# Cross-attention and expert FFN on one core: which score tiles are multiplied in three rounded terms, who copies the shift row, and the order of the last sums

## What is computed

```python
kv = context @ Wkv;  k, v = split(kv);  q = layernorm(x) @ Wq
dots = einsum('bhnd,bhmd->bhnm', q, k) * SCALE
dots = dots - (1.0 - mask)[:, None, :, None] * 1000000.0
attn = softmax(dots, axis=-1)
x = x + (einsum('bhnm,bhmd->bhnd', attn, v) heads merged) @ Wout + bout
# then: x = x + ffn(layernorm(x)), one expert (w1, b1, gelu, w2, b2) for each batch
```

## Time and profile before

| what | value |
|---|---|
| median of 3 executions | 381.06 us (379.85 to 382.0) |
| profiled execution, its time | 381.56 us |
| profiled execution, span of the trace | 379.6 us |
| mean granted TensorE clock | 0.991 of full speed |
| PE, DVE, ACT, POOL busy | 367.0, 278.7, 255.1, 115.5 us |

### The profile page before, as it was taken

The page is one execution under the profiler, slowest core; times in us unless marked ns, Lnnn a source line. Parts: engine busy times, 40 slices in busy tenths (PEclk is TensorE's granted clock), DMA queues, the critical chain, the costliest instruction groups (busy, mean ns, idle before and its releaser), DMA issues.

```text
span 379.6 us, 5788 instructions
## 1 busy us (share of the span) xinstructions
PE 367.0 (97%) x1713; PEld 280.4 (74%) x1713; DVE 278.7 (73%) x456; ACT 255.1 (67%) x334; POOL 115.5 (30%) x125
## 2 busy tenths in 40 slices
PE   7899999999999999999999999999999999999795
PEld 6667777777777787777767887777777887787555
DVE  5888577977797679787698579686789678443653
ACT  3556576797679467796679466887688466958321
POOL 1701562245225341226123431336133330022000
PEclk9999999999999999999999999999999999999988
DMA  7587277348734673359735493279636550377000
GB/s 243 202 191 174 54 145 178 85 116 157 180 82 112 115 179 57 96 130 248 169 96 126 90 205 75 59 164 230 160 92 141 93 100 10 106 147 133 12 2 6
DMA packets 30622, 47.10 MB, mean 124 GB/s; under 512 B 2011, under 2 KB 21371, under 8 KB 30608
## 3 DMA queue, kind: packets, MB, share of 16 engines
q0 software_dynamic: 9936, 27.40, 37.0%
q1 hardware_dynamic: 20672, 19.52, 17.2%
HBM read 24.59 MB, written 0.23 MB: 65 GB/s over the span
## 4 chain that ended last, share of the span: by engine, by line
PE 83%; DVE 10%; issue 3%; DMA 2%; ACT 1%; SPq 1%; DVEq 0%
PE ps_s L439 27%; PE ps_a L479 22%; PE ps_x L496 10%; PE ps_a L472 9%; PE ps_x L529 4%; PE ps_a L416 2%; PE ps_x L549 2%; DMA ctxt_raw<-in_ctx_t 2%; DVE ex_sum L889 2%; DVE shift_diag L910 1%; PE ps_x L453 1%; DVE chunk_max L899 1%; PE ps_x L558 1%; DVE ex_lo L895 1%; PE ps_x L509 1%
## 5 line engine op out<-in xcount | busy, mean ns | idle before, releaser
L899 DVE TENSOR_REDUCE chunk_max<-ps_x 128x1 f32<-128x500 f32 x168 | 110.9, 676 | 31.2 <-PE ps_x L496 28.3
L697 ACT ACTIVATE ex_all<-ps_s 125x896 f32<-125x896 f32 x96 | 88.0, 917 | 46.3 <-PE ps_s L439 44.6
L479 PE MATMUL ps_a<-ex_all,ctx_sb 125*128 125x448 f32 x248 | 110.9, 540 | 0.0
L715 ACT COPY ps_s<-shift_row 125x896 f32<-125x896 f32 x94 | 85.7, 911 | 12.6 <-DVE shift_row L1036 10.0
L496 PE MATMUL ps_x<-ctxt_hi,qk_hi 128*128 128x500 f32 x168 | 80.3, 481 | 1.7 <-DVE chunk_max L899 1.5
L1213 POOL DMA_DIRECT2D ex_all<-ex_all x48 | 42.2, 879 | 117.5 <-ACT ex_all L697 113.3
L439 PE MATMUL ps_s<-qk_hi,ctxt_hi 128*125 128x448 f32 x192 | 76.3, 479 | 0.0
L479 PEld LDWEIGHTS ps_a<-ex_all,ctx_sb 125*128 125x128 f32 x248 | 46.2, 189 | 16.8 <-issue 12.4
L439 PE MATMUL ps_s<-qk_hi,ctxt_lo 128*125 128x448 f32 x192 | 54.8, 367 | 0.0
L439 PE MATMUL ps_s<-qk_lo,ctxt_hi 128*125 128x448 f32 x192 | 54.7, 366 | 0.0
L439 PEld LDWEIGHTS ps_s<-qk_hi,ctxt_hi 128*125 128x125 f32 x192 | 35.9, 187 | 24.5 <-issue 23.4
(11 more groups left out here) (108 smaller groups left out, 385.4 us busy)
## 6 DMA issues: line engine op xcount, KB each, us to landing
ex_all<-ex_all POOLq DMA_DIRECT2D x48, 448.0 KB, 4.5
ctxt_raw<-in_ctx_t SPq DMA_DIRECT2D x8, 750.0 KB, 6.1
ctx_sb<-in_ctx SPq DMA_DIRECT2D x8, 750.0 KB
ctxt_hi<-in_ctx_t POOLq DMA_DIRECT2D x21, 250.0 KB, 3.0
w_sb<-in_w SPq DMA_DIRECT2D x4, 512.0 KB, 4.7
...
```

What stands on the lines that cost most here:

```text
L479: mm = nc.tensor.matmul(ps_a[:, c, 0:CH], ctx_sb[0:MT, u, t, :], ex(t)[0:MT, c * CH:(c + 1) * CH], start=(slot == 0), stop=(slot == TM - 1))
L697: nc.scalar.activation(half(ex(t)[0:MT, :]), src, ACT.Exp, scale=SCALE).then_inc(ex_ready, 1)
L715: nc.scalar.copy(ps_s[0:MT, t % 2, :, 0:CH], half(shift_row[0:MT, b.parity, :])).then_inc(seeded, 1)
L899: nc.vector.tensor_reduce(chunk_max[:, k, t:t + 1], filled()[:, 0:MC], AX.X, ALU.max).then_inc(job_free, 1)
```

## The change

- `SPLIT` becomes 0, 2, 4, 6, 8, 10: tiles 0 and 10 are multiplied in three rounded terms too, except tile 10 of the last batch. `ctx_hi` and `ctx_lo` hold six context tiles instead of four. `PV_ORDER` swaps its last two tiles, so tile 10 takes slot 11.
- The row sum is made as 0+9, +1, +10, +2, +11 (`SUM_PARTS`). The first addition is at (10, 2), the next two at (11, 1), the last two again at the start of the next batch.
- DVE's two copies of the shift row are gone. ACT copies both banks of `ps_x` at once into `ps_s` as the seed of the first tile (`first_seed`), then into `shift_row`, and only then counts both banks as drained. For batch 0 that seed is tile 2's.
- ACT rounds the row sum after the next batch's exponential of tile 1 instead of tile 0; it goes into `shift_diag`, no longer a buffer of its own.
- In the last batch additions come at (10, 0) and (11, 0), the first half of `last_probs_ctx` stands ahead of the sum's products, and `y_job` of half 0 uses the form that half 1 had: even heads in 64 rows of the bank, odd heads in the other 64, and one more addition on DVE to join them.
- In batch 0 `ctx_hi` is made by ACT during the setup, `ctx_lo` by POOL in step 0.

The diff, without the lines that only rename or delete a helper's body:

```diff
-    SUMS = CHAINS - 1 + TM - 1 - LAST_DMA
-    SPLIT = [2, 4, 6, 8]
-    PV_ORDER = [0, 1, 2, 3, 5, 4, 7, 6, 9, 8, 10, 11]
+    SUM_PARTS = [9, 1, 10, 2, 11]
+    SUMS = len(SUM_PARTS)
+    SPLIT = [0, 2, 4, 6, 8, 10]
+    PV_ORDER = [0, 1, 2, 3, 5, 4, 7, 6, 9, 8, 11, 10]
...
-    ADD_AT = {(10, 2): (0,), (11, 0): (1, 2)}
+    ADD_AT = {(10, 2): (0,), (11, 1): (1, 2)}
     ADD_LATE = (3, 4)
-    LAST_ADD_AT = {(10, 2): (0,), (11, 0): (1, 2), (11, 1): (3,)}
+    LOW_AT = [(t + 1, 1) for t in SPLIT[:-1]] + [(11, 0)]
+    LAST_ADD_AT = {(10, 0): (0, 1), (11, 0): (2, 3)}
...
-        sum_hi = sb("sum_hi", [P, Q], F32R)
+        sum_hi = shift_diag[:, :, :].rearrange("p t q -> p (t q)")
...
+        def buffer_free(n):
+
+            return read_by(SPLIT[n - 2]) if n >= 2 else read_by(SPLIT[SPLITS - 2 + n]) - TM
+
+        def summed(t):
+
+            return 1 + (SUM_PARTS.index(t) if t else 0)
...
-            def last_probs_ctx(b):
-
-                pe.wait_ge(ex_ready, b.at(TM, TM))
-                for c in range(2):
-                    for t in (TM - 2, TM - 1):
-                        mm = nc.tensor.matmul(ps_a[:, c, 0:CH], ctx_sb[0:MT, b.parity, t, :], ex(t)[0:MT, c * CH:(c + 1) * CH],
-                                              start=False, stop=(t == TM - 1))
-                    mm.then_inc(last_half, 1)
+            def last_probs_ctx(b, c):
+
+                for t in (TM - 2, TM - 1):
+                    pe.wait_ge(ex_ready, b.at(TM, t + 1))
+                    mm = nc.tensor.matmul(ps_a[:, c, 0:CH], ctx_sb[0:MT, b.parity, t, :], ex(t)[0:MT, c * CH:(c + 1) * CH],
+                                          start=False, stop=(t == TM - 1))
+                mm.then_inc(last_half, 1)
...
-                    if pair.half == 1:
+                    if pair.half is not None:
                         out_rows = slice(TOK * (h % 2), TOK * (h % 2) + TOK)
...
+            last_probs_ctx(last, 0)
             sum_jobs(last)
-            last_probs_ctx(last)
+            last_probs_ctx(last, 1)
...
+            def first_seed(b, t):
+
+                act.wait_ge(job_ready, jobs.value())
+                act.wait_ge(ex_ready, b.at(TM, t - 1))
+                nc.scalar.copy(ps_s[0:MT, t % 2, :, 0:CH], ps_x[0:MT, :, 0:CH]).then_inc(seeded, 1)
+                nc.scalar.copy(half(shift_row[:, b.parity, :]), ps_x[:, :, 0:CH]).then_inc(job_free, 2)
...
                     exponentials(b, t)
                     if t == 1 and b.off > 0:
+                        sum_high_part(b.later(-1))
                         att_out(b.later(-1))
-                    if t + 2 < TM:
-                        if t == 0 and first:
-                            jobs.n += 2
+                    if prepare and t == TM - 2:
+                        ex_high_part(b, SPLITS - 1)
+                    if t == 0 and first:
+                        jobs.n += 2
+                        first_seed(b, 2)
+                    elif t + 2 < TM:
+                        if t == 1 and first:
                             act.wait_ge(job_free, jobs.value())
                         seed(b, t + 2)
                     elif prepare:
                         if t + 2 == TM:
                             jobs.n = FIRST_JOBS if first else jobs.n + 2
+                            first_seed(b.later(1), 0)
+                        else:
                             act.wait_ge(job_free, jobs.value())
-                        seed(b.later(1), t + 2 - TM)
-                    if t == 0 and b.off > 0:
-                        sum_high_part(b.later(-1))
+                            seed(b.later(1), 1)
...
-                    if t in SPLIT:
+                    if t in SPLIT[:-1]:
                         ex_high_part(b, SPLIT.index(t))
...
+                if h == HEADS - BEHIND:
+                    ctx_high_part(Batch(None, 0))
                 drain_later_queries(h)
...
-                if pair.half == 1:
+                if pair.half is not None:
+                    other = slice(TOK * (1 - pair.half), TOK * (1 - pair.half) + TOK)
                     step(nc.vector.tensor_tensor(x1[r, :], bank[r, 0:D], pair.pick(x_tok)[r], ALU.add))
-                    nc.vector.tensor_tensor(x1[r, :], bank[0:TOK, 0:D], x1[r, :], ALU.add).then_inc(job_free, 1)
+                    nc.vector.tensor_tensor(x1[r, :], bank[other, 0:D], x1[r, :], ALU.add).then_inc(job_free, 1)
...
-            def shift_copies(b):
-
-                wait(dve, seeded, b.at(TM, -TM - 2))
-                for c in range(2):
-                    nc.vector.tensor_copy(shift_row[:, b.parity, c * CH:(c + 1) * CH], filled()[:, 0:CH]).then_inc(job_free, 1)
...
-                    if (at[0] - 1, at[1]) in [(t, 1) for t in SPLIT]:
-                        ex_low_part(b, SPLIT.index(at[0] - 1))
+                    if at in LOW_AT and (prepare or LOW_AT.index(at) < SPLITS - 1):
+                        ex_low_part(b, LOW_AT.index(at))
...
-                        pool.wait_ge(ex_lo_ready, b.at(SPLITS, 2))
+                        pool.wait_ge(ex_lo_ready, b.at(SPLITS, 3))
```

More of the change, by code:

```diff
@@ L472, in probs_ctx @@
                             mm = nc.tensor.matmul(ps_a[:, c, 0:CH], a[0:MT, u, n, :], e[0:MT, n % 2, c * CH:(c + 1) * CH],
-                                                  start=False, stop=False)
+                                                  start=(slot == 0 and term == 0), stop=(slot == TM - 1 and term == 2))
                     mm.then_inc(pv_done, 1)
@@ L562, in shift_jobs @@
             def shift_jobs():
-                for c in range(2):
+                for _ in range(2):
+                    c = jobs.n % 2
                     shift_rows(job()[:, 0:CH], P, c, start=True).then_inc(job_ready, 1)
@@ L687, in exponentials @@
                 if t < CHAINS:
-                    wait(act, ex_summed, b.at(SUMS, max(t, 1) - SUMS))
+                    wait(act, ex_summed, b.at(SUMS, summed(t) - SUMS))
                 elif t < CHAINS + RING:
@@ L692, in exponentials @@
                     if before > LAST_DMA:
-                        wait(act, ex_summed, b.at(SUMS, CHAINS - 1 + before - LAST_DMA - SUMS))
+                        wait(act, ex_summed, b.at(SUMS, summed(before) - SUMS))
                 else:
@@ L702, in ex_high_part @@
                 act.wait_ge(ex_ready, b.at(TM, t + 1))
-                if n >= 2:
-                    act.wait_ge(pv_done, b.at(TM, read_by(SPLIT[n - 2])))
+                wait(act, pv_done, b.at(TM, buffer_free(n)))
                 nc.scalar.copy(ex_hi[0:MT, n % 2, :], ex(t)[0:MT, :]).then_inc(ex_hi_ready, 1)
@@ L877, in add_to_sum @@
             def add_to_sum(b, n):
+                t = SUM_PARTS[n]
                 dst = ex_sum[0:MT, b.parity, :]
[L880 to L883 removed]
+                left = ex(0)[0:MT, :] if n == 0 else dst
+                if n == 0:
+                    added_by_dma(dve, b, LAST_DMA - CHAINS + 1)
+                if t < CHAINS:
+                    added_by_dma(dve, b, LAST_DMA - CHAINS + 1 + t)
                 else:
[L885 removed]
                     dve.wait_ge(ex_ready, b.at(TM, t + 1))
[L887 removed]
                 wait(dve, ex_summed, b.at(SUMS, n))
[L889 removed]
+                nc.vector.tensor_tensor(dst, left, ex(t)[0:MT, :], ALU.add).then_inc(ex_summed, 1)
             def ex_low_part(b, n):
                 dve.wait_ge(ex_hi_ready, b.at(SPLITS, n + 1))
[L894 removed]
+                wait(dve, pv_done, b.at(TM, buffer_free(n)))
                 nc.vector.tensor_tensor(ex_lo[0:MT, n % 2, :], ex(SPLIT[n])[0:MT, :], ex_hi[0:MT, n % 2, :].bitcast(F32),
@@ L1045, in drain @@
                 def drain(at):
-                    if b.off == 0 and at == FIRST_SHIFT_AT:
-                        shift_copies(b)
-                    if prepare and at == SHIFT_AT:
-                        shift_copies(b.later(1))
+                    if (b.off == 0 and at == FIRST_SHIFT_AT) or (prepare and at == SHIFT_AT):
+                        jobs.n += 2
                     if b.off == 0 and at in FOLD_AT:
@@ L1223, in iteration @@
                 for t in range(TM):
-                    if b.i is None and b.off == 0 and t == 2:
+                    if b.i is None and b.off == 0 and t == 0:
                         ctx_low_part(b)
```

12 lines of the change are left out of this document (1 added, 11 removed).

## The result

The changed kernel takes 379.34 us (median of 10 runs, 378.34 to 379.68), the kernel before 380.98 (10 runs, 379.85 to 382.64). The ratio is 0.9949, 95% interval 0.9931 to 0.9967. So 1.6 us were gained where 4.6 were forecast; the time lies just above the range. The profiled execution of after took 379.52 us (span 377.6), 2.04 less than that of before.

What follows compares the result with a forecast made beforehand. PE, busy 97% of the span and 83% of the chain, was taken as the bound. Terms summed to -4.8 us: 376.8 on the profiled execution's 381.56, 376.3 for the median, forecast as 376.5, range 374.0 to 379.3.

Steps and rivals of the forecast that it cites:

- Tiles: Tiles 0 and 10 on PE: 15 tiles in three rounded terms, 1.23 us each instead of 1.50, -4.05 us.
- Row copy and third reduction in batch 0: Batch 0: PE waits 1.6 us for ACT's two copies and 0.7 for a reduction behind `ex_lo`, +2.3 us.
- Moved `ctx_lo`: Batch 0's setup: GpSimd's earlier subtraction had no term in the prediction's sum.
- Slot 0: Batches 1 to 6: PE's job in tile 0's slot waits 0.2 us for a reduction behind `ex_lo`, +1.2 us.
- Tile 2's slot: The job at 121.65, started by DVE's chain behind the row sum: PE and ACT both come earlier, nothing taken.
- first rival: Batches 1 to 6: helpers take back PE's lead at the job at 121.65, 2.0 us lost, 378.5 us; chance 0.20.
- Order of the operands: Row sum: tile 2's buffer comes fourth, ending waits for its DMA transfer in batch 3, -0.4 us once.
- `att`: Last batch: ACT rounds the sum ahead of the `att` copy, so PE comes later, +0.25 us.
- Projection and tail: Last batch: half 0's projection in the other form, -1.4 us; reordered tail without PE's wait before the sums, -2.7.
- Clock: New tail: no term in the sum; as a rival, half speed from the projection on, +1.3 us, 377.8; chance 0.15.
- "slower" rival: DVE falls behind PE at every batch's end, 1.0 us passed on in each of 7 batches, 383.3 us; chance 0.05.

Runs made afterwards that it cites:

- E12: The kernel before with only the row sum's five operands in the new order, additions at their old places: 380.62 us, ratio 0.9978.
- E8: The changed kernel with VectorE's subtraction of `sum_lo` one reduction later in every batch: 377.78 us, ratio 0.9911.
- E2: The changed kernel with batch 0's shift row copied by VectorE in two halves and tile 2 seeded from that row: 377.49 us, ratio 0.991.
- E1: The changed kernel with GpSimd's `ctx_lo` of batch 0 held until the shift is written: 377.92 us, ratio 0.9924.
- E5: The changed kernel with GpSimd's first `ctxt_lo` of each batch held until VectorE has written `ex_lo` of tile 2: 379.26 us, ratio 0.9951.
- E3: The kernel before with only `ctx_hi` and `ctx_lo` of batch 0 (four tiles) made as early as in the changed kernel: 381.64 us, ratio 1.0022.
- E4: The kernel before with only the new order of additions and the reordered last batch, including the new projection of half 0: 376.68 us, ratio 0.9889.
- E11: The changed kernel with the old last batch: late additions, last products behind the sums, old projection of half 0: 383.80 us, ratio 1.0065.

## Why the prediction was wrong

- *Tiles, -4.05: right.* 1.23 and 1.51 in the chain. Between E12 and E8 an even batch shortens by 0.33, and 0.21 more of waiting came in (0.20 + 0.11 for 0.10 at the job in tile 2's slot): 0.54, two tiles of 0.27. The odd ones shorten by 0.44, batch 1 by 0.24 with 0.26 of waiting at its shift job.
- *Row copy and third reduction in batch 0, +2.3: right in mechanism, 0.5 short.* Batch 0 grew by 2.55 although tile 0 gave 0.27: +2.8. Each wait costs more than its idle time, which I had not added: the starts are late by 1.85 + 0.08 and 0.85 + 0.11 us, for waits of 1.69 and 0.68. E2 shows the copy's part.
- *Moved `ctx_lo`: the step that failed.* The sum has no term for it, which puts it at nothing without a reason. It held VectorE's smallest operation on the path to the first exponential, +1.2 (E1: 1.4 by the medians). The Trainium skill states the rule (SBUF — State Buffer, "SBUF: two separate sides"): VectorE and GpSimd share a pair of ports under an exclusive lock, and when a VectorE operation with two SBUF inputs meets a GpSimd operation that reads SBUF, the one that starts first has the ports to its end and the other is blocked. The traces agree: L928 has two SBUF inputs, started after `ctx_lo` and ended 0.03 us after it. I asked of each moved operation what waits for it, and not what runs beside it.
- *Slot 0, +1.2: right, a little small.* 0.24 (odd) to 0.27 (even) a batch, 1.55. E8 takes it away whole (1.56).
- *Tile 2's slot, 0: the second step that failed.* I saw that the job at 121.65 was VectorE's, and asked what ScalarE's chain would do. But `sum_lo` comes a whole `ex_lo` later, GpSimd starts behind it, and its `ctxt_lo` lands on `ex_lo` of tile 2. +0.70 in the three even batches by the traces of after and E5; the medians don't show it. So the first rival's place was right, for another reason.
- *Order of the operands, -0.4:* -0.45 by the medians (not certain), -1.36 between two profiles. Before's waits for the transfer differ between executions: E3, with the old order, has 44.31 in b4, where before has 44.77. And 0.26 of the -1.36 is the shift job's wait in b1, which is back in after.
- *`att`, +0.25:* PE's slot 0 of the last batch starts 0.54 late, and 0.06 more; before had 0.08 there. +0.5.
- *Projection and tail, -4.1: right, the size in part by luck.* 3.94 by E12 and E4. The forecast took the sums' saving of 1.5 us from one trace with the lower clock and called it sure. In the profiles of E3 and E11 the old tail, after the same wait, ran its sums at the full clock in 1.77 us; from E11's 60.93 to after's 58.23 projection and tail together are worth 2.70, or 3.1 without after's 0.4 of lower clock.
- *Clock, 0 in the forecast:* +0.4 in the profile of after (58.23 against E8's 57.82); it came in the hidden layer, and not in every execution. In the profile of E4, with the same tail, it came in the projection, where the rival put it (16 matmuls in 1.61 us for 1.09). It cost 0.55 there, not 1.3, as the wait behind it shrank.

Against the profile: -4.8 + 0.5 + 1.2 + 0.35 + 0.70 - 0.96 + 0.25 + 0.4 = -2.4, with 0.5 of a longer set-up -1.9; measured -2.04. (The 0.26 of b1 and the projection of half 0, 0.27 better than its term of 1.4, are left out; they cancel.) What decided the miss are the 1.9 us of two GpSimd operations on VectorE's time: 1.2 shown by E1, 0.7 by stages alone. The "slower" rival (VectorE late at each batch's end) did not come: ScalarE's cast, seed and row copy end at 108.88 after batch 1's end, 0.05 ahead of the next exponential, and VectorE's wait for the cast of tile 10 is 0.24 us (E1's trace).
